# GNN with four layers on one core: GpSimd's bursts of indirect DMAs get further waits

## The reference

```python
src, dst = ...          # 206250 edges, both directions and self loops, sorted by dst
x = layernorm(x + L0(x, edge_attr_8))     # per edge: silu(x_src (x) e (x) W) W2, summed at a node
x = layernorm(x + L1(x))                  # six graph convolutions with the normalised adjacency
x = layernorm(x + L2(x, edge_weight1))    # segment_max(x[src] * t, dst) @ W.T + b
x = layernorm(x + L3(x, edge_attr_13))

# L3, NREPEATS = 2, nc = 16
w = relu(edgefeats @ fnet_w1 + fnet_b1) @ fnet_w2 + fnet_b2
W = w.reshape(-1, nc, nc)                 # a 16 x 16 matrix for every edge
for _ in range(NREPEATS):
    m = einsum('ei,eio->eo', hx[edge_src], W)
    agg = segment_sum(m, edge_dst) * inv_deg[:, None]
    hx = gru_cell(agg, hx)
```

## Time and profile before

| | us |
|---|---|
| median of 3 runs | 11252.9 (11231.1 to 11258.11) |
| the profiled execution, its own time | 11253.09 |
| its span | 11251.3 |
| pass 0, about | 325 to 3267 |
| passes 1 to 6, about | 3300 to 5100 |
| pass 7, about | 5142 to 6882 |
| pass 8, about | 7039 to 9050 |
| pass 9, about | 9200 to 11205 |
| busy: PE | 8897.2 (79%) |
| busy: PEld | 5698.2 (51%) |
| busy: DVE | 6144.4 (55%) |
| busy: POOL | 4484.3 (40%) |
| busy: ACT | 3561.2 (32%) |

### The profile page before, as it was taken

One profiled execution on the slowest core, in us unless ns is written; L12 is line 12 of the kernel. 1 busy time (PEld: TensorE's weight loads), 2 busy tenths in 40 slices (PEclk: granted clock), 3 DMA queues, 4 the chain that ended last, 5 costly groups with the idle time before them and its releaser, 6 DMA issues. The chain is left out here.

```text
span 11251.3 us, 211389 instructions
## 1 busy us (share of the span) xinstructions
PE 8897.2 (79%) x72779; PEld 5698.2 (51%) x72910; DVE 6144.4 (55%) x11833; ACT 3561.2 (32%) x10701; POOL 4484.3 (40%) x4575
## 2 busy tenths in 40 slices
PE   0588888888878999956888885888788858788887
PEld 0345544555556878843444443555444535455544
DVE  2577766777753232223555553665666636666666
ACT  4234322333320010002444443333333323333334
POOL 1455555556530000005444553444444334444442
PEclk9899988899986999957888887888888878888888
DMA  9422233222239878973555553333333423333333
GB/s 317 151 76 81 80 86 88 80 80 80 80 122 368 311 251 313 337 310 116 157 158 159 159 159 108 109 105 106 107 105 108 113 68 105 108 105 107 106 107 90
DMA packets 998418, 1625.38 MB, mean 144 GB/s; under 512 B 253394, under 2 KB 787598, under 8 KB 997174
## 3 DMA queue, kind: packets, MB, share of 16 engines
q1 hardware_dynamic: 808244, 1542.53, 41.8%
q0 software_dynamic: 146240, 27.89, 3.0%
q10 hardware_dynamic: 43202, 44.90, 1.2%
HBM read 1324.07 MB, written 289.76 MB: 143 GB/s over the span
## 5 line engine op out<-in xcount | busy, mean ns | idle before, releaser
L841 POOL DMA_INDIRECT arena<-tab,x_all x2902 | 2747.6, 947 | 5074.9 <-DMA tab<-stage 2026.1
L859 POOL DMA_INDIRECT adj<-acc x1616 | 1683.0, 1041 | 1288.5 <-DVE acc L1933 747.2
L900 PE MATMUL ps<-invdeg,acc 128*128 128x384 bf16 (+1 forms) x5377 | 1369.2, 413 | 224.1 <-issue 216.2
L900 PE MATMUL ps<-dinv,acc 128*128 128x384 bf16 (+1 forms) x5404 | 1267.9, 387 | 324.5 <-issue 259.0
L1310 ACT ACTIVATE wide<-ps,not_all 128x128 bf16<-128x128 f32 x1616 | 658.2, 419 | 1535.6 <-remote 993.0
L900 PEld LDWEIGHTS ps<-invdeg,acc 128*128 128x128 bf16 x5454 | 621.3, 120 | 939.7 <-issue 738.7
L900 PEld LDWEIGHTS ps<-dinv,acc 128*128 128x128 bf16 x5454 | 591.0, 114 | 962.1 <-issue 745.6
L1493 ACT ACTIVATE arena<-w_iota,rel 128x128 f32<-128x128 f32 x3232 | 987.9, 388 | 13.5
L2287 DVE TENSOR_TENSOR dinv<-ps,arena 128x512 f32<-128x512 f32 x808 | 519.1, 684 | 784.6 <-remote 778.8
L2287 DVE TENSOR_TENSOR arena<-ps,arena 128x512 f32<-128x512 f32 x808 | 519.2, 684 | 725.8 <-remote 708.6
L1499 ACT ACTIVATE acc<-arena,unit 128x1024 bf16<-128x1024 f32 x303 | 347.9, 1148 | 1744.4 <-PE ps L1238 894.6
(11 more groups left out here) (357 smaller groups left out, 14006.6 us busy)
## 6 DMA issues: line engine op xcount, KB each, us to landing
arena<-adj SPq DMA_DIRECT2D x588, 896.0 KB, 5.6
arena<-rels SPq DMA_DIRECT2D x202, 512.0 KB
arena<-tab SPq DMA_DIRECT2D x1616, 64.0 KB
invdeg<-hot_rows_of SPq DMA_DIRECT2D x150, 672.0 KB
dinv<-hot_rows_of SPq DMA_DIRECT2D x100, 896.0 KB
adj<-zero SPq DMA_DIRECT2D x28, 3136.0 KB
dinv<-hot_rows_of SPq DMA_DIRECT2D x102, 672.0 KB
x_all<-src_parts SPq DMA_DIRECT2D x202, 256.0 KB
```

The costliest lines, as they stand in the source:

```text
L841: pool.indirect_dma_start(G[b][:, u, :], None, TABLE[PHASES[p]], bass.IndirectOffsetOnAxis(ap=idx[:, t:t + 1], axis=0)).then_inc(gathered[ ...
L859: pool.indirect_dma_start(adj_cells, bass.IndirectOffsetOnAxis(ap=pair[:, t, 0:1], axis=0), pair16[:, t, 2:3], None).then_inc(celled[g], 16)
L900: mm(rows, x8[:, b, i, :], hots[:, b, :], start=b == i == 0, stop=False)
```

## The change

GpSimd's bursts wait for more. In passes 8 and 9, the burst for batch k (from k = 16 on) also waits until VectorE has done the select that stands in iteration k - 16, the one of batch k - 12 (`selected[p]` at k - 16 + AHEAD + 2), and until TensorE has made the second half of the W products of batch k - 15. In pass 0, the burst of batch k also waits until TensorE has finished the message sums of batch k. Nothing else is touched: no instruction is added on another engine, and every engine keeps its order.

```diff
@@ -832,6 +832,9 @@
                 b = k % len(G)
                 if p > 7:
                     pool.wait_ge(vec[p].sem, vec[p].at(max(k - len(G), -SL), USED))
+                    if k >= len(G):
+                        pool.wait_ge(selected[p], min(k - len(G) + AHEAD + 2, NB))
+                        pool.wait_ge(ten[p].sem, ten[p].at(k - len(G) + 1, WT8_LATE))
                 elif k == len(G):
                     pool.wait_ge(vec[p].sem, vec[p].at(0, 0))
                 else:
@@ -851,6 +854,7 @@
             pool.wait_ge(adj_zeroed, 16 * ZEROS)
             for k in range(NB):
                 pool.wait_ge(vec[0].sem, vec[0].at(k, COUNTED))
+                pool.wait_ge(ten[0].sem, ten[0].at(k, TPER[0]))
                 for i in range(R):
                     for g in range(HT // R):
                         t = k * HT + g * R + i
```

## The result

The changed kernel takes 11004.06 us (median of 3, 10994.05 to 11009.58), against 11252.9: a ratio of 0.977, 95% interval 0.975 to 0.979, 249 us faster. The forecast was a gain of 478 us.

A forecast was written before the change was run, and what follows sets the result against it. The prediction held that TensorE's signals wait out GpSimd's bursts, 10.26 us per batch in passes 8 and 9. From 11253.1, less 540 there, plus 60 in pass 0, it forecast 10775 us, range 10430 to 11330.

The forecast's parts named there:

- What bounded passes 8 and 9: Passes 8 and 9: TensorE's signals inside a burst reach other engines only behind it; 10.26 us per batch, 6.2 without bursts.
- The period there: Passes 8 and 9: 8.8 us per batch after the change instead of 10.25, saving 540 us over 372 bursts.
- the sum: Whole kernel: 11253.1 less 540 for passes 8 and 9 plus 60 for pass 0, giving 10775 us.
- The middle of 8.8: Passes 8 and 9: value taken between 8.0 us, clock stretch covered by the burst, and 9.6, whole period stretched.
- The reaction: Passes 8 and 9: the burst starts 0.27 us after the select.
- The register load: Passes 8 and 9: TensorE's load L878 falls some 0.7 us into the new burst and passes, costed at nothing.
- the slower rival: Passes 8 and 9: register load held until 7.2 us into the burst, 10.8 us per batch, 11518 us in all; chance 0.14.
- Signal passes: Pass 0: first `compare`'s signal gets out early in the burst, 14.0 us per batch; weighted 7 to 3 against held.
- TensorE's gaps late in a burst: Pass 0: TensorE's stops during its round inside the burst, taken as 1.9 us per batch.
- both cases: Pass 0: first `compare`'s signal passes, 14.0 us, or is held, 16.5 us; weighted 7 to 3, 14.75 against 14.43.
- the gap of one row: Pass 0: one "issue" stop of TensorE of 1.05 us, the basis for the 1.9 us taken with smaller ones.
- The rule on ports: Skill's rule: only VectorE and GpSimd's shared port pair contends, TensorE never waits; moving bursts would give nothing, 11253 us.

The follow-up runs named there:

- e3_w_only: Kernel before, but bursts of passes 8 and 9 also wait for the W products, not for the select; pass 0 as before: 10813.16 us, ratio 0.959.
- d1_one_dma: Kernel before with 1 gathering DMA per batch instead of 4 or 5 in passes 8 and 9, leaving work out: 9644.53 us.
- r_order: Changed kernel with the wait on TensorE written first, so that it stands on the first DMA itself: 10761.40 us, ratio 0.970 to before.
- h_after: Kernel before with only pass 0's changed wait and 4 of its 8 cell DMAs per batch, half the cells unwritten: 10310.64 us.
- the second group: Runs on one chip, kernel before 11061.16 us: one wait on TensorE in passes 8 and 9, half of pass 0's cell DMAs, or one gathering DMA per batch.
- e5_again: Kernel before, but bursts of passes 8 and 9 wait only for the W products, not the last product; pass 0 as before: 10651.92 us, ratio 0.961.

## Why the prediction was right in sign and half in size

- **What bounded passes 8 and 9.** Right. Signals of TensorE reached the others behind the burst, and moving the burst gives 483 us by the trace and 475 alone, against 540 forecast.
- **The period there.** Forecast 8.8, measured 8.96. The working was off: I had the burst chained to the select by way of the picked rows' signal. In truth that signal is out early, and the W products come last (e3_w_only alone does it). TensorE's round, which the sum put at 5.9 us, or 7.1 with the clock, and hid under the burst of 7.28, takes 8.25 us busy and 0.70 us stopped and sets the period alone. The stops I had seen in pass 0 and not counted here. At a clock of 1.00 the round is 6.2 us (d1_one_dma), and 6.2 / 0.86 is 7.2, so 1 us of the busy time stays unexplained. The middle of 8.8 that I took for the clock happened to lie near; that is luck.
- **The reaction.** The burst starts 3.7 us behind the select and not 0.3 (medians). I took a reaction of 0.27 us from the one-wait burst; with the waits of the change it is 0.78 behind the W products. r_order shows that this difference is hardly worth anything here.
- **The register load** passes early in a burst, as argued; the slower rival did not come.
- **Pass 0, the step that failed.** "Signal passes: the round of 11.8, plus TensorE's gaps late in a burst [...] I take 1.9 [...]: 14.0 us." The signal did pass. The term mis-sized is the gaps: between the second `compare` and the burst's end TensorE does almost nothing, and a third of the sums (2.8 us, more at the lower clock) comes behind. Measured 15.7 us: 11.9, some 3.0 for what is left of the sums, and 0.76. So the case I held for the likelier one came, and still cost 1.7 us more than its 14.0. With the mean over both cases at 14.75 the sum had a loss of 60 us; it was 239 to 249. The gain is half of the forecast because passes 8 and 9 nearly kept theirs and pass 0 lost four times what the sum had for it. I had taken the gap of one row for the rule, where a longer stay of the round in the burst multiplies them. h_after shows the other side: the same round without the last four DMAs has no gap and takes 10.5 us.
- **The rule on ports** is not borne out as a full account: in the second group a batch takes 9.7 us with four or five DMAs and 6.2 with one, and VectorE's sum hardly differs (2.28 and 2.27 us). The Trainium skill (SBUF — State Buffer, Who interferes with whom) says that TensorE never waits on anyone, which may hold of the ports that it speaks of; the runs show that TensorE's signals, loads and matmuls do wait in a burst.

What the runs don't settle is why TensorE stops late in a burst. "Issue" says only that nothing recorded was waited for. That its instructions come late by the same path that holds its signals was argued, not shown. How much of the price of a burst is the lower clock, and whether the stops bring the clock down, no run separates. Nor is it known why the groups differ in the kernel before (10.26 and 9.71 us per batch in pass 8).

## What to carry to other kernels

Read which engine's signals are late while another one issues indirect DMAs, and put the burst where the engine that is hit has the most work that nobody waits for yet. Here the length of the burst mattered more than its place. One DMA cost nothing that shows, four in pass 0 left no stop in TensorE, and eight stopped it for 2.5 us per batch (495 us in pass 0). When the burst is out of the way, ask again what bounds the stage: here it was TensorE's own round, and an earlier burst gave little. A wait that moves a burst should be tried in each stage by itself, since here two parts of one change had opposite signs.

## What the runs showed of the hardware

- TensorE's signals in mid-burst came out only 11.9 us after the start of a burst of eight indirect DMAs (0.97 us each with 0.30 between) and 7.3 us after that of five (0.94 us each), while those of its first 3 us nearly all passed at once (160 of 162 within 2 us, in pass 0 after). VectorE's signals to ScalarE passed 3 to 6 us into a burst.
- A register load of TensorE that fell due in mid-burst started only at the end of the burst of five, about 7.2 us in (161 of 184 loads of pass 8 before); in the first 1.25 us of a burst it ran at once (155 of 184 after).
- In bursts of eight TensorE stopped between matmuls from about 7 us on, 0.9 us at a time and up to 1.9 (495 us in pass 0), and in a series of sixteen DMAs from 8 us on to its end (e5_again). In the bursts of four or five of pass 8 after the change the stops came 3 to 7 us in (125 us of them). With bursts of four in pass 0 there was none.
- A burst began 0.27 us after the signal it waited for where that wait stood on the DMA (r_order), and 0.78 us where it stood on a wait instruction ahead of it (after; medians of pass 8). That instruction has a record there, EVENT_SEMAPHORE L837, 0.74 us before the DMA.
- The same kernel before took 11268 and 11061 us in two groups of runs with the same chip number.
